# LayerNorm and residual loads at other places of the SP queue, and weight pieces in other slots, in an attention plus ternary FFN kernel on eight cores

## What is computed

```python
x = x + attn(layernorm(x), Wqkv, Wproj, bproj)      # 16 heads of 64; scores over the heads of one token
x = x + ffn(layernorm(x), w_gate, w_up, w_down)
# attn: q, k, v per token and head; softmax(q k / 8) over the 16 heads g of the same token; out @ Wproj + bproj
# ffn:  bitlinear(silu(bitlinear(x, w_gate)) * bitlinear(x, w_up), w_down)
# bitlinear: activations rounded to 8-bit steps per row, weights to -1, 0, 1 times the mean of |w|
```

## Time and profile before

| | |
|---|---|
| median of 3 runs | 3935.33 us |
| the three runs | 3935.33, 3819.6, 3935.67 us |
| profiled execution, time | 3841.83 us |
| its span on the slowest core (7) | 3840.3 us |
| spans of the eight cores | 3813.2 to 3840.3 us |
| share of the span busy: PE, weight loads, DVE, ACT, POOL | 97%, 53%, 69%, 23%, 7% |
| DMA engines busy, attention stage | six to seven tenths of the time in most slices, nine at the start |

### The profile page before, as it was taken

One profiled execution on the slowest core, in us unless ns is written; L12 is line 12 of the kernel. 1 busy time (PEld: TensorE's weight loads), 2 busy tenths in 40 slices (PEclk: granted clock), 3 DMA queues, 4 the chain that ended last, 5 costly groups with the idle time before them and its releaser, 6 DMA issues.

```text
span 3840.3 us, 89704 instructions; the slowest of 8 cores (3813.2 to 3840.3 us)
## 1 busy us (share of the span) xinstructions
PE 3708.8 (97%) x35554; PEld 2051.4 (53%) x35554; DVE 2668.6 (69%) x4445; ACT 879.5 (23%) x1474; POOL 262.2 (7%) x386
## 2 busy tenths in 40 slices
PE   6999999999998899999999999999999999999999
PEld 5777777767776344444444444444444444444444
DVE  2433457667765587877777777777777777777776
ACT  2655553333333111111111111111111111111110
POOL 1111112111221000000000000000000000000000
PEclk9999999999999999999999999999999999999999
DMA  9767656665655533333333333333323233333332
GB/s 185 205 198 205 196 172 175 191 189 159 179 178 151 168 61 78 84 69 66 67 86 77 69 69 68 87 72 69 72 74 80 70 72 69 75 86 72 67 66 80
DMA packets 436762, 427.61 MB, mean 111 GB/s; under 512 B 349504, under 2 KB 355904, under 8 KB 435776
## 3 DMA queue, kind: packets, MB, share of 16 engines
q1 hardware_dynamic: 396752, 300.22, 31.2%
q0 software_dynamic: 39600, 121.66, 12.3%
HBM read 264.51 MB, written 79.69 MB: 90 GB/s over the span
## 4 chain that ended last, share of the span: by engine, by line
PE 92%; DMA 3%; issue 2%; DVE 1%; DVEq 1%; ACT 0%; SPq 0%; POOL 0%; ACTq 0%; POOLq 0%
PE pb L533 23%; PE pb L545 23%; PE pb L599 18%; PE pb L435 16%; PE pb L514 6%; PE pb L564 1%; PE pb L417 1%; PE pb L494 1%; PE pb L437 1%; PE pb L476 1%; PE pb L458 1%; DMA x_ln<-x 1%; DMA wqkv_sb<-wqkvT 1%; DMA stage<-wuT 1%; PE pb L451 0%
## 5 line engine op out<-in xcount | busy, mean ns | idle before, releaser
L533 PE MATMUL pb<-wg,xq_fm 128*128 128x512 fp8e4 x4096 | 970.6, 380 | 12.7 <-DMA xq_fm<-xq_tm 12.5
L545 PE MATMUL pb<-wu,xq_fm 128*128 128x512 fp8e4 x4096 | 968.3, 379 | 0.0
L713 ACT ACTIVATE silug<-pb,agm 128x512 f32<-128x512 f32 x512 | 351.9, 687 | 2174.7 <-PE pb L533 2174.7
L435 PE MATMUL pb<-xn_fm,wqkv_sb 128*64 128x256 bf16 x6144 | 754.5, 279 | 34.4 <-issue 20.5
L437 PE MATMUL pb<-xn_fm,wqkv_sb 128*64 128x256 bf16 x6144 | 755.4, 279 | 6.7 <-issue 6.7
L435 PEld LDWEIGHTS pb<-xn_fm,wqkv_sb 128*64 128x64 bf16 x6144 | 658.7, 112 | 88.1 <-issue 64.9
L887 DVE SCALAR_TENSOR_TENSOR m<-pb,agm,silug 128x512 f32<-128x512 f32 x512 | 383.6, 749 | 419.0 <-PE pb L545 414.1
L533 PEld LDWEIGHTS pb<-wg,xq_fm 128*128 128x128 bf16 x4096 | 400.8, 98 | 498.1 <-issue 18.0
L437 PEld LDWEIGHTS pb<-xn_fm,wqkv_sb 128*64 128x64 bf16 x6144 | 658.5, 112 | 10.9 <-issue 10.9
L545 PEld LDWEIGHTS pb<-wu,xq_fm 128*128 128x128 bf16 x4096 | 401.0, 98 | 484.1 <-issue 1.6
L599 PE MATMUL pb<-wd,hq_fm 128*128 128x512 fp8e4 x1920 | 470.8, 379 | 1.1 <-DVE outb L920 1.1
(11 more groups left out here) (87 smaller groups left out, 2476.4 us busy)
## 6 DMA issues: line engine op xcount, KB each, us to landing
x_ln<-x SPq DMA_DIRECT2D x64, 512.0 KB, 7.7
stage<-wgT POOLq DMA_DIRECT2D x64, 512.0 KB, 5.6
x_res<-x SPq DMA_DIRECT2D x64, 512.0 KB, 11.0
xnew_scr<-x_res SPq DMA_DIRECT2D x64, 512.0 KB, 6.7
stage<-wuT POOLq DMA_DIRECT2D x64, 512.0 KB, 5.5
stage<-wdT POOLq DMA_DIRECT2D x64, 512.0 KB, 4.8
xnb<-xnew_scr SPq DMA_DIRECT2D x64, 512.0 KB, 4.1
outb<-xnew_scr SPq DMA_DIRECT2D x64, 512.0 KB, 5.3
```

Source lines behind the costliest of these rows:

```text
L435: t.matmul(bank[0:64, hh * 256:(hh + 1) * 256], w, xf[:, m * 512:m * 512 + 256], start=(m == 0), stop=(m == 7))
L533: ins = t.matmul(PG[jg % 2][:], xq_fm[k % 2][:, m * 128:(m + 1) * 128], wg_sb[pc][:, m * 512:(m + 1) * 512], start=(m == 0), stop=(m == 7))
L545: ins = t.matmul(PU[jg % 2][:], xq_fm[k % 2][:, m * 128:(m + 1) * 128], wu_sb[pc][:, m * 512:(m + 1) * 512], start=(m == 0), stop=(m == 7))
L713: sc.activation(silug[jg % 2][:], PG[jg % 2][:], AF.Silu, scale=agm[:, 2 * (k % 2):2 * (k % 2) + 1]).then_inc(SM["a_silu"], 1)
```

## The change

The SP queue issues `load_ln` and `load_res` at other places of its loop, and both slot lists for the weight pieces are changed. Nothing is computed differently, and the number of DMAs is the same.

```diff
-SUM_SLOTS = (0, 1, 3, 4, 6, 7, 9, 10, 12, 13, 15, 16, 18, 19, 21, 22)
+SUM_SLOTS = (1, 3, 4, 5, 6, 7, 8, 9, 10, 11, 12, 13, 14, 15, 16, 18)
-QUANT_SLOTS = (1, 4, 6, 8, 10, 12, 13, 15, 16, 18, 19)
+QUANT_SLOTS = (1, 4, 6, 8, 9, 10, 12, 13, 14, 15, 16)
@@ sync_body
                     if it >= 1 and c in (12, 17):
                         for s in ((0, 1) if c == 12 else (2, 3)):
                             store_new(it - 1, s)
-                    if it + 2 < nt and c in (14, 15):
-                        for s in ((0, 1) if c == 14 else (2, 3)):
-                            load_ln(it + 2, s)
-                    if 1 <= it < nt and c in (18, 22):
+                    if 1 <= it and it + 1 < nt and c in (0, 2):
+                        for s in ((0, 1) if c == 0 else (2, 3)):
+                            load_ln(it + 1, s)
+                    if 2 <= it < nt and c in (4, 7):
+                        for s in ((0, 1) if c == 4 else (2, 3)):
+                            load_res(it - 1, s)
+                    if 1 <= it and it == nt - 1 and c in (18, 22):
                         for s in ((0, 1) if c == 18 else (2, 3)):
                             load_res(it, s)
```

## The result

The changed kernel is slower by about one per cent: the ratio of its time to that of the kernel before is 1.0106, 95% interval 1.0075 to 1.0136, that is 41 us. The medians over all executions, 3885.03 and 3885.02 us, show none of this, because in some executions of either kernel the cores of one half of the chip, or of both, run at a lower granted clock and take some per cent longer; all comparisons here leave those out, or keep to cores 4 to 7 where only these ran as usual. The profiled execution took 3876.17 us, 34 us more than the one before (3841.83). Its slowest core is core 4 with a span of 3874.6 us; the mean over the eight cores' spans rose from 3830 to 3855.7 us.

A forecast was written before the change was run, and what follows sets the result against it. PE, 92% of the chain, was taken to lose 5.94 us per iteration to late instruction packets in slots 17 to 23. +12 us there and -4 at the start gave +8 on 3841.8: 3850 us, range 3803 to 3950.

The forecast's parts named there:

- What bounds the kernel: Slots 17 to 23: instruction packets come late behind data transfers; 5.94 us lost per iteration, nearly nothing elsewhere.
- The SP order: From slot 17 SP issues 1 MB stores, 2 MB x_ln, 2 MB x_res in a row, in iterations 1 to 13.
- The price in slots 17 to 23: Slots 17 to 23: DMA work rises from 18.2 to 19.9 us per iteration, taken as +12 us over 13 iterations.
- The second bound: Slots 17 to 23: price from iteration 14's extra load, 0.72 us per us of DMA work; +16 us over 13 iterations.
- The third bound: Slots 17 to 23: loss grows with what is queued at once, 5 MB for 3 MB; +51 us over 13 iterations.
- The pieces at cost 0: Weight pieces moved to earlier slots cost nothing there: taken as 0, at most 0.5 us per iteration for ScalarE.
- Part 2: The prediction's step on slot lists: pieces leaving slots 17 to 23 save 3.6 us DMA work per iteration, cost 0 elsewhere.
- No data wait follows: x_ln and x_res loads issued from slot 17 land in 7.7 and 11.0 us, needed 36 us after issue; no wait.
- The start: Before iteration 1: 2 MB of x_ln leave the time before PE's Wqkv wait; gain 4 us, later delay taken 0.
- A (the backlog decides): Slots 17 to 23: instruction packets wait behind all 5 MB, gaps grow; 3889 us, chance 0.25, 0.10 for 2% slower.
- B (the pieces were the harm): Slots 17 to 23: POOL's weight-piece transfers delay instruction packets, so fewer pieces take half the loss along; 3799 us, chance 0.14.
- C: Loads really leave slots 17 to 23, nearly all loss is regained, 77 us and the start; about 3761, chance 0.03.

The follow-up runs named there:

- held_all_again: Kernel before, with x_res rows 0, 1 loaded behind x_ln, rows 2, 3 held until next slot 8, second store pair until next slot 0; ratio 0.9854.
- loads_only: Changed kernel with the old slot lists, so that only the SP order differs from the kernel before; ratio 1.0078.
- stage_small: Kernel before with each weight piece after the first two loaded with 128 of 1024 columns; profiled execution 3780.79 us, one run only.
- lists_only: Kernel before with only the two changed slot lists, loads of x where they were; ratio 1.0121.
- held_text: Changed kernel with the old slot lists and waits on PE's progress holding x_ln loads until slots 0 and 2, x_res until 4 and 7; ratio 0.9938.

## Why the prediction was right and wrong

**What bounds the kernel: right.** The loss was 5.94 us per iteration in slots 17 to 23, from transfers and dense instructions together. held_all_again recovers 76.45 - 72.36 = 4.1 us of it. That the late things are the instruction packets themselves was argued, and no run alters those packets alone, but the traces show it. PE has 74137 instructions for 289 packets, so each carries 256. In iterations 1 to 13 of the kernel before, the eight cores have 230 gaps over 0.25 us with no semaphore pending. Of the 168 on the six cores with complete records, 158 begin at the very same place, 187 instructions past a multiple of 256, and of all 230, 206 end 1.2 to 1.65 us after the end of an instruction packet, where 7% of random moments would. In the changed kernel it is 205 of 209 and 260 of 275. No wait of the program is tied to such a place. Counting packets from 0, packet k begins on average when PE is 249 instructions past 256 k with no x transfer in flight, and 353 past it with four. The latest begins at 443, which is 256 + 187: where PE stands still.

**The SP order: right.** 5 MB in a row from the end of slot 16, DMA share 0.57 to 0.6 forecast for slots 12 to 16 and 0.58 to 0.73 read in the twelve iterations of core 4 (0.65 over all cores), 0.85 or more forecast for slots 17 to 23 and 0.79 to 0.95 read (0.86).

**The price in slots 17 to 23: right in size, by luck.** +12 us was the term. Averaged over the cores the stretch is 24.58 us long instead of 23.55, 1.03 us per iteration, 13 us over 13. But the term is the difference of two others. At its price, 12 / 13 / 1.7 = 0.54 per us of DMA work, the 5.3 us of `x_ln` cost 37 us and the 3.6 us of pieces give back 25. The runs put other numbers there. In this stretch DMA work was 18.5 us before, 22.6 in loads_only and 21.2 in the changed kernel, so +4.1 and -1.5. The stretch is 0.73 us longer in loads_only, and with the lists on top it grows by 0.30 us where it should have shrunk. Of the 0.93 us of idle time that the change adds here, 0.38 are waits for ScalarE and VectorE, which the forecast had at nothing.

The second bound, 0.72 per us, rested on one iteration of one core. Averaged over the cores iteration 14 spends 23.78 us in these slots, against 23.55 in the thirteen before it, so core 7's 3.1 us were mostly scatter. The third bound, +51 by what is queued at once, was void. With 4, 5, 6 and 7 x transfers in flight in the changed kernel packet k begins when PE is 376, 391, 388 and 384 instructions past 256 k. That count cannot exceed 443, where PE stands still, so I also took the time since PE passed 256 k, which has no such ceiling: 9.9, 10.4, 9.4 and 8.9 us, against 5.8 with none in flight. The wait does not grow beyond four. The Trainium skill ("DMA: Bandwidth & Descriptors", Queues, rings and completion order) leads one to expect this, since an engine takes turns between queues packet by packet.

**The pieces at cost 0: wrong, and this is the step that failed.** Part 2 put what they cost where they go at 0, and what their leaving saves at 3.6 us of DMA work per iteration, 25 us in all by the price above. By the times, the loads alone (loads_only) cost 30 us, where the forecast's terms for them give 37 - 4 = 33; adding the lists costs 11 more, where the forecast had 25 less. The loads were 3 us cheaper than forecast and the lists 36 us dearer, which together is the miss of 33. Part 2 said that DVE idles 1.76 and 2.87 us before `pj_ev`, so that a piece of 2.03 us fits, and that ScalarE would wait "a few times" under cover of the projections. I compared engine time with idle time, and used one median landing, 5.5 us, for the piece's own load. What counts is when the buffer comes free: the read two pieces earlier, then 0.7 and 0.6 us of POOL issue, then a landing that under the stores of slot 12 takes 7.6 us. The run that has only the lists loses 46 us. In the changed kernel idle time in slots 0 to 16 rose by 0.66 us per iteration, 0.55 of it waits for other engines; in iterations 7 to 13 slot 15 alone has 0.72 us.

**"No data wait follows", and the spill: half right.** No engine waits for `x_ln` or `x_res` loads. But the burst ends later than I worked out. It runs into the next iteration: idle time is 0.36 us in slot 0 of iterations 7 to 13 (0.14 before) and 0.61 us in slot 2 of iterations 1 to 6 (0.04 before). These slots hold 31 to 33 PE instructions per us, fewer than the score slots, so the rate of a single slot does not decide it; slots 22 and 23, just ahead of them, have 41 to 57. I had counted gaps in slots 17 to 23 only.

**The start: half right.** Iteration 0 is 2.4 us shorter (4 forecast), and PE's wait for the last block of Wqkv is one of 4.3 us instead of two of 10.5 together (averaged over the cores, 4.1 instead of 9.7 us of waits for Wqkv). But iteration 1 is 3.0 us longer, of which 1.1 lie in slots 0 to 11 and 1.9 in slots 17 to 23; of the 0 to +4 I had taken 0. Which part of that comes from the `x_ln` loads of tile 2 behind the copy of the projection weights is not shown: iteration 1 is 4.4 us longer with the loads alone and 5.6 us with the lists alone.

**The sum.** By iterations of the two traces: -2.4 in the first, 1.93 x 13 = +25.1 in the next thirteen, +2.2 in iteration 14, that is +25, which is the rise of the mean span (25.8 us). The forecast was +8. Of the missing 17, the thirteen iterations hold 11.7 outside slots 17 to 23 (25.1 - 13.4): 8.6 are idle time, pieces and spill together, and the remaining 3.1 stay open. One is in slots 17 to 23, 1.6 in iteration 0, and 2.2 in iteration 14, which I had not counted. The ratio of the times, 1.0106, is +41 us, and the cores' mean span shows as much when all comparable executions are taken, 3858 against 3812 us. The traces fall short of that because the one of the kernel before is a long one; in which slots its shorter executions save their time, no trace shows.

**The rivals.** A (the backlog decides) was right in sign and wrong in mechanism. B (the pieces were the harm) is half true, as stage_small shows. Taking two or three of them out of the score slots did help PE's instructions along: in lists_only, gaps with no semaphore pending in slots 17 to 23 fell from 3.34 to 2.14 us per iteration. But waits for other engines there rose from 0.13 to 2.03 us. In the changed kernel the 2 MB of `x_ln` took the pieces' place, and the gaps with no semaphore pending are 3.89 us. C, forecast at 3761 us if the loads really left, came to 24 us gained in held_text rather than 77, because the early slots got gaps of their own; held_all_again gained 56.

## What to carry to other kernels

A queue that is programmed slot by slot goes by its semaphores: an issue moved to a later place in the text is made earlier or later only if a wait there holds it. Put large transfers where the other engines' instructions are few and long, and count DMA work per stretch, all queues together, before moving any of it. A load behind two buffers has to land within two of its consumers' slots, and the time to compare is its landing in that stretch, not the consumer's idle time.

## What the runs showed of the hardware

PE can be starved of instructions by data transfers: gaps of up to 5.6 us in slots 17 to 23, with no semaphore pending, in a stretch of 44 instructions per us at a DMA share of 0.8 and more, and nearly none in one of 31 per us with a share of 0.97. Nine in ten of these gaps end 1.2 to 1.65 us after an instruction packet has, and in the kernel before 158 of 168 begin at the same instruction of a block of 256. The lateness of a packet does not grow with the number of x transfers in flight beyond four, and the loss is steep in the load: taking away nearly all of the weight pieces, or of the `x_res` loads, removes about 70 or 80% of the idle time in the stretch (3.47 to 1.01 and to 0.63 us).
